# ScalarE writes x plus normed x, GpSimd adds the bias behind its gathers, and x2 is transposed at the end of the outer layer

## The chip, the cores and the metric

The kernel runs on one core of one Trainium2 chip. The metric is device time in microseconds (us); lower is better. The core's engines are TensorE (PE in the rows; PEld is its weight load), VectorE (DVE), ScalarE (ACT), GpSimd (POOL) and SyncE (SP), each with its own instruction stream, and they order themselves by semaphores. ACTq and SPq are the places where ScalarE and SyncE issue transfers.

## The reference

A graph layer and then a mixture-of-experts layer run over 6250 nodes of 256 features and 100000 edges of 96 features, all in float32:

```python
# graph layer, on xn = layernorm(x)
out1 = segment_sum(edge_attr, dst);  out2 = segment_max(edge_attr, dst) (0 where a node has no edge)
out3 = out1 / max(count, 1)
h = concat([xn, out1, out2, out3, u[0]])
x = x + (relu(h @ W1 + b1) @ W2 + b2) + xn
# expert layer, on x2 = layernorm(x): 16 experts, the best two by x2 @ gate_w + gate_b
x = x + layernorm(x2 + moe(x2)) * gamma + beta
```

The part that matters here is the sum behind the graph layer: for each node row it adds the product with W2, the bias b2, the row x and its normed row xn.

## The kernel before

Three stages follow each other. In the first, DVE scans the edges in ten chunks, each 96 + 96 scans, and SyncE stores the running sums and maxima of a chunk to DRAM. In the second, the outer layer, the 6250 nodes are taken in 25 macro steps of 250 nodes (two tiles of 125 rows), from the last node to the first. The third routes the nodes and runs 113 expert tiles. The first and second overlap: macro step i needs the chunks that hold the last edges of its nodes, and the semaphore chunk_done says how many are stored.

Each engine runs a macro step as a hand-written order of helper calls, and what it works on differs from engine to engine:

- PE, gnn_step(i): layer1(i) in two halves of four hidden blocks (lines 969, 971, 973), with router(i-2) between the halves (line 1002); turn(i+1), which transposes the inputs of the next step (lines 950, 953); layer2(i), 32 + 32 recorded matmul rows for its two tiles (line 983), with turn_x2(i-1), four transposes (line 995), between the tiles.
- ACT, gnn_step(i): store_x1(i-1), which waits for the finished rows; moments1(i+1), the mean and deviation of the next x (lines 734, 739); carry_in(i+1), the scaling and masks of what the gathers brought (lines 717 to 725); relu(i, 0) (line 769); take_logits(i-2) (line 810); moments2(i-1) (lines 778, 783); the issue of the load of x for step i+2 (line 743); mask_rows(i+1), which ends with the normed x in XN (lines 749 to 755); relu(i, 1); take_turned(i+1); write_x2(i-1) and its store (lines 791, 801); take_x2(i-1) (line 806); take_g(i), which copies layer2's result out of PSUM (line 817).
- POOL, rows_step(i): add_rows(i-1), GO = GO + RES (line 549); residual(i), which is RES = XN + x (line 566) and then RES = RES + b2 (line 568); cut(i+1) (line 527); norm1(i+1) (lines 540 to 544); join(i+1) (lines 531 to 535); norm2(i-1) (lines 554 to 559); gather(i+2), an index copy (line 512) and six indirect transfers (lines 520 to 522).

RES is one buffer. XN, XR (the raw x) and the gathered tiles have two buffers each. PE's wait that matters most below is in the second half of layer1(i), which takes over the PSUM banks that relu(i, 0) has read:

```python
if q:
    pe.wait_ge(h_ready, (i + 1) * HC + n + 1)
```

Of the kernel before, what the change touches and what calls it, by code (L numbers as in the profile page):

```python
# [21 lines left out]
ALU = mybir.AluOpType  # L22
ACT = mybir.ActivationFunctionType
# [59 lines left out]
def after(i, g, b, n=1):  # L83

    return i + n, g + (b + n) // 2, (b + n) % 2


def gnn_moe_kernel(nc, x, dst, edge_attr, u, gW1, gb1, gW2, gb2, gate_w, gate_b,
# [5 lines left out]
    NX, _, FF = ew1.shape  # L94
    NT = 125
    TILES = N // NT
    MACROS = TILES // 2
# [58 lines left out]
    with ExitStack() as ctx:  # L156
        def sem(name):
            return ctx.enter_context(nc.semaphore(name))
# [7 lines left out]
        k = Area(mem, 0, KEPT)  # L166
# [22 lines left out]
        wsel = k.take(2, TILES, parts=NT)  # L189
        IX = k.take(TILES, 2, parts=NT, dt=U32)  # L190
        rowU = k.take(TILES, parts=NT, dt=U32)
        mean1, dev_1, rstd_1, nmr_1 = (k.take(2, parts=NT) for _ in range(4))
        Lo = k.take(TILES, NX, parts=NT)
        gatef = k.take(MACROS, parts=1)
        gatei = k.take(MACROS, parts=1, dt=I32)
# [128 lines left out]
        pick_step = sem("pick_step")  # L324
        ix_copied, carried, joined, node_rows = sem("ix_copied"), sem("carried"), sem("joined"), sem("node_rows")
        xr_got = [sem(f"xr_got{i}") for i in range(2)]
        residual_ready, x1_ready = sem("residual_ready"), sem("x1_ready")
        moments2_step, norm2_step, rstd2_ready = sem("moments2_step"), sem("norm2_step"), sem("norm2_rstd_ready")
        turned, turned_out = sem("turned"), sem("turned_out")
        h_psum, h_ready, g_psum, g_out = sem("h_psum"), sem("h_ready"), sem("g_psum"), sem("g_out")  # L330
# [138 lines left out]
        def _(pool):  # L469
# [39 lines left out]
            def gather(i, g, b):  # L509
                level = pool.value_load(gatei[0:1, bass.ds(MACROS - 1 - i, 1)], min_val=1, max_val=LEVELS)  # L510
                hold(pool, turned, i + 1)
                pool.tensor_copy(IXn[b], IX[:, bass.ds(2 * (MACROS - 1 - i), 2), :]).then_inc(ix_copied, 1)
                pool.wait_ge(ix_copied, i + 1)
                hold(pool, chunk_done, level * LEVEL)
                for lv in range(1, LEVELS + 1):
                    edges, pieces = lv * LEVEL * P * T, lv * LEVEL * P
                    with pool.If(level == lv):
                        for a in range(2):
                            last, before = (bass.IndirectOffsetOnAxis(IXn[b][:, a, n:n + 1], 0) for n in range(2))
                            pool.indirect_dma_start(out=GM[b][:, a, :], out_offset=None, in_=s_max[0:edges], in_offset=last).then_inc(gathered[b], 16)  # L520
                            pool.indirect_dma_start(out=GS[b][:, a, :], out_offset=None, in_=s_sum[0:edges], in_offset=last).then_inc(gathered[b], 16)
                            pool.indirect_dma_start(out=GC[b][:, a, :], out_offset=None, in_=carry[0:pieces], in_offset=before).then_inc(gathered[b], 16)
# [11 lines left out]
                pool.wait_ge(picked, i + 1)  # L534
                pool.tensor_tensor(RAW[b][:, :, 1, :], take_c, take_p, ALU.add).then_inc(joined, 1)

            def norm1(i):
                s2 = Steps(pool, norm1_step, i * 2)
                hold(pool, moments1_step, i * 4 + 4)
                s2.mark(pool.tensor_scalar(dev_1, dev_1, 1.0 / D, EPS, ALU.mult, ALU.add))  # L540
                s2.wait()
                s2.mark(pool.tensor_tensor(rstd_1, dev_1, rpow, ALU.pow))
                s2.wait()
                pool.tensor_tensor(nmr_1, mean1, rstd_1, ALU.mult).then_inc(rstd1_ready, 1)

            def add_rows(i):
                pool.wait_ge(g_out, i + 2)
                pool.wait_ge(residual_ready, 2 * i + 2)
                pool.tensor_tensor(GO, GO, RES, ALU.add).then_inc(x1_ready, 1)

            def norm2(i):
# [6 lines left out]
                hold(pool, norm2_step, i * 2 + 2)  # L558
                pool.tensor_tensor(nmr_2[:, at], mean2, rstd_2[:, at], ALU.mult).then_inc(rstd2_ready, 1)

            def residual(i, g, b):
                if not isinstance(i, int) or i:
                    pool.wait_ge(x1_ready, i)
                pool.wait_ge(xr_got[b], (g + 1) * 16)
                pool.wait_ge(node_rows, i + 1)
                pool.tensor_tensor(RES, XN[b], XR[b][0:NT], ALU.add).then_inc(residual_ready, 1)
                pool.wait_ge(residual_ready, 2 * i + 1)
                pool.tensor_tensor(RES, RES, b2bc, ALU.add).then_inc(residual_ready, 1)

            def rows_step(i, g, b):  # L570
                more = not isinstance(i, int) or i + 1 < MACROS
                norm = not isinstance(i, int) or i >= 1
                if norm:
                    add_rows(i - 1)
                residual(i, g, b)
                if more:
                    cut(*after(i, g, b))
                    norm1(i + 1)
                    join(*after(i, g, b))
                if norm:  # L580
                    norm2(i - 1)
                if not isinstance(i, int) or i + 2 < MACROS:
                    gather(*after(i, g, b, 2))
            pool.sem_inc(joined, 1)
            gather(0, 0, 0)
            norm1(0)
            cut(0, 0, 0)
            join(0, 0, 0)
            gather(1, 0, 1)
# [62 lines left out]
        def _(act):  # L652
# [89 lines left out]
            def load_x(i, b):  # L742
                act.dma_start(XR[b], node_rows_of(MACROS - 1 - i)).then_inc(xr_got[b], 16)

            def mask_rows(i, g, b):
                act.wait_ge(joined, i + 2)
                for a in range(2):
                    j = bass.ds(2 * (MACROS - 1 - i) + a, 1)
                    act.activation(NB[b][:, a, 0:2 * EF], RAW[b][:, a, :, :].rearrange("p s f -> p (s f)"), ACT.Identity, scale=has[:, j])
                    act.activation(NB[b][:, a, 2 * EF:2 * P], RAW[b][:, a, 0, 0:EF - REST], ACT.Identity, scale=rch[:, j])  # L750
                    act.activation(NB[b][:, a, 2 * P:3 * P].rearrange("p (n r) -> p n r", n=QUAD), spread(RAW[b][:, a, 0, EF - REST:EF], 1, QUAD),
                                   ACT.Identity, scale=rch[:, j])
                act.wait_ge(rstd1_ready, i + 1)
                for a in range(2):
                    ins = act.activation(XN[b][:, a, :], XR[b][0:NT, a, :], ACT.Identity, bias=nmr_1[:, a:a + 1], scale=rstd_1[:, a:a + 1])  # L755
                ins.then_inc(node_rows, 1)

            def take_turned(i, g, b):
                act.wait_ge(turned, i + 3)
# [39 lines left out]
            def store_x2(i):  # L799
                act.wait_ge(x2_rows, i + 1)  # L800
                act.dma_start(by_pair(x2_d)[bass.ds(MACROS - 1 - i, 1)], X2p).then_inc(x2_st, 16)
# [18 lines left out]
            def gnn_step(i, g, b):  # L820
                more = not isinstance(i, int) or i + 1 < MACROS
                norm = not isinstance(i, int) or i >= 1
                logit = not isinstance(i, int) or i >= 2
                if norm:
                    store_x1(i - 1)
                if more:
                    moments1(*after(i, g, b), 0)
                    moments1(*after(i, g, b), 1)
                    carry_in(*after(i, g, b))
                relu(i, 0)  # L830
                if logit:
                    take_logits(i - 2)
                if norm:
                    moments2(i - 1, 0)
                    moments2(i - 1, 1)
                if not isinstance(i, int) or i + 2 < MACROS:
                    act.wait_ge(residual_ready, 2 * i + 2)
                    load_x(i + 2, b)
                if more:
                    mask_rows(*after(i, g, b))  # L840
                relu(i, 1)
                if more:
                    take_turned(*after(i, g, b))
                if norm:
                    write_x2(i - 1)
                    store_x2(i - 1)
                    take_x2(i - 1)
                take_g(i, g, b)
            moments1(0, 0, 0, 0)
            moments1(0, 0, 0, 1)  # L850
            act.wait_ge(index_ready, 1)
# [66 lines left out]
        def _(pe):  # L918
# [56 lines left out]
                    if between and q == 0:  # L975
                        between()

            def layer2(i, g, b, between=None):
                for a in range(2):
                    for hc in range(HC):  # L980
                        if a == 0 and (hc == 0 or hc > QUAD):
                            pe.wait_ge(h_ready, (i + 1) * HC + max(hc, QUAD) + 1)
                        ins = pe.matmul(bank(5, a * D, (a + 1) * D, NT), H[:, hc, a * NT:(a + 1) * NT], W2[:, hc, :], start=(hc == 0), stop=(hc == HC - 1))  # L983
                    if between and a == 0:
                        between()
                ins.then_inc(g_psum, 1)

            def turn_x2(r):
# [17 lines left out]
            def gnn_step(i, g, b):  # L1006
                layer1(i, g, b, (lambda: router(i - 2)) if not isinstance(i, int) or i >= 2 else None)
                if not isinstance(i, int) or i + 1 < MACROS:
                    turn(*after(i, g, b))
                layer2(i, g, b, (lambda: turn_x2(i - 1)) if not isinstance(i, int) or i >= 1 else None)  # L1010
            turn(0, 0, 0)
            gnn_step(0, 0, 0)
            gnn_step(1, 0, 1)
# [398 lines left out]
```

## Time and profile before

| | us |
|---|---|
| median of three runs | 1420.55 |
| lowest and highest of them | 1414.31, 1423.67 |
| the profiled execution | 1423.21 |
| its span, first to last instruction | 1421.5 |
| PE, DVE, ACT, POOL busy | 1201.3, 848.0, 645.1, 795.2 |
| outer layer, first PE transpose to last router | 121.82 to about 789 |

The first row is the time that a change is held against; the profiled execution is one run, 2.7 us above it, and 1.7 us of it lie outside its span. The busy sums run over stages with different limits, so they don't say what a macro step waits for. This is read from the order of the rows within a step.

### The profile page before, as it was taken

To read this page: it belongs to the slowest core of one execution; us is meant where nothing else is said; L and a number is where in the kernel's file an instruction comes from. 1 tells how busy PE (TensorE), PEld (TensorE's weight loads), DVE (VectorE), ACT (ScalarE), POOL (GpSimd) and SP (SyncE) were. 2 spreads that over 40 slices of the span, in tenths; PEclk is the share of its full clock that TensorE was granted. 3 is DMA by queue.
4 is the path that set the end of the run, shared out by engine and by line. 5 is a ranking of instruction groups with operands and counts; after the bars stand their busy time and mean duration, and the time that the engine had idled before them with its cause. 6 is when DMAs were issued, how large, how long until landed. Compare 5 with 4: busy or idle time off the path is not lost.

```text
span 1421.5 us, 28692 instructions
## 1 busy us (share of the span) xinstructions
PE 1201.3 (85%) x6677; PEld 1015.0 (71%) x6678; DVE 848.0 (60%) x3007; ACT 645.1 (45%) x1969; POOL 795.2 (56%) x1060
## 2 busy tenths in 40 slices
PE   2004998998998999999998254999999999999798
PEld 1003887887887788788887144999999999998343
DVE  5999999999999899000000695344444344443796
ACT  5853555656656556566563000332323232323453
POOL 4874565665665566666751001676766777765122
PEclk7556999999999999999999577999999999999555
DMA  9976677676676656611110823122221222222883
GB/s 314 300 227 246 232 268 268 265 276 262 258 281 260 230 186 236 196 45 42 58 34 30 278 85 133 62 69 74 69 71 63 75 69 71 69 72 58 297 284 102
DMA packets 87468, 231.48 MB, mean 163 GB/s; under 512 B 22145, under 2 KB 34819, under 8 KB 87285
## 3 DMA queue, kind: packets, MB, share of 16 engines
q1 hardware_dynamic: 50401, 167.53, 32.5%
q0 software_dynamic: 26048, 43.47, 10.5%
q10 hardware_dynamic: 10964, 19.96, 4.0%
q14 instruction: 47, 0.39, 0.1%
q8 instruction: 8, 0.13, 0.0%
HBM read 116.42 MB, written 114.25 MB: 162 GB/s over the span
## 4 chain that ended last, share of the span: by engine, by line
PE 54%; DVE 33%; DMA 4%; issue 4%; POOL 2%; ACT 1%; DVEq 1%; SPq 0%; POOLq 0%; ACTq 0%
PE ps L1061 14%; PE ps L1069 14%; DVE mem L1142 12%; DVE mem L1146 12%; PE ps L983 5%; PE ps L969 5%; PE ps L971 5%; PE ps L1089 3%; PE ps L1091 3%; PE ps L1048 2%; DVE mem L1162 2%; DVE mem L1283 1%; DMA mem<-piece_carry,mem 1%; DMA mem<-in_edge_attr_dram 1%; DVE mem L1167 1%
## 5 line engine op out<-in xcount | busy, mean ns | idle before, releaser
L879 ACT ACTIVATE mem<-ps,mem 128x128 f32<-128x128 f32 x452 | 128.8, 368 | 374.8 <-PE ps L1061 374.8
L969 PE MATMUL ps<-mem 128*128 128x250 f32 x800 | 214.1, 391 | 27.2 <-ACT mem L769 25.7
L1061 PEld LDWEIGHTS ps<-mem 128*128 128x128 f32 x1808 | 221.8, 194 | 5.7
L1061 PE MATMUL ps<-mem 128*128 128x128 f32 x1808 | 222.2, 277 | 0.0
L1069 PE MATMUL ps<-mem 128*128 x904 | 213.8, 379 | 0.4 <-issue 0.4
L1142 DVE TENSOR_TENSOR_SCAN mem<-ps,mem 128x80 f32<-128x80 f32 x960 | 207.9, 303 | 0.3
L971 PE MATMUL ps<-mem 128*128 128x250 f32 x800 | 208.1, 383 | 0.0
L1146 DVE TENSOR_TENSOR_SCAN mem<-ps,mem 128x80 f32<-128x80 f32 x960 | 207.8, 308 | 0.0
L621 POOL DMA_INDIRECT expert_rows<-mem x113 | 138.2, 1223 | 113.3 <-DVE mem L1317 66.0
L969 PEld LDWEIGHTS ps<-mem 128*128 128x128 f32 x800 | 156.2, 198 | 47.5 <-ACT mem L769 27.4
L983 PE MATMUL ps<-mem 128*125 128x256 f32 x800 | 180.9, 379 | 0.7 <-ACT mem L769 0.7
L1069 PEld LDWEIGHTS ps<-mem 128*128 128x128 f32 x904 | 163.0, 190 | 18.3 <-issue 0.7
L971 PEld LDWEIGHTS ps<-mem 128*128 128x128 f32 x800 | 156.8, 196 | 19.8
L983 PEld LDWEIGHTS ps<-mem 128*125 128x125 f32 x800 | 146.2, 188 | 21.0 <-ACT mem L769 1.1
L1317 DVE TENSOR_TENSOR mem<-ps,mem 128x256 f32<-128x256 f32 x113 | 47.9, 424 | 170.0 <-PE ps L1069 166.9
L1310 DVE COPY mem<-mem 128x1024 f32 x113 | 78.4, 694 | 85.0 <-issue 81.8
L1232 DVE TENSOR_TENSOR mem<-mem 125x800 f32<-125x800 f32 x1 | 1.0, 994 | 214.0 <-ACT mem L810 214.0
L615 POOL DMA_INDIRECT mem<-x_normed,mem x113 | 113.4, 1004 | 24.1 <-issue 16.9
L950 PE MATMUL ps<-mem 125*128 125x125 f32 x100 | 20.7, 289 | 94.4 <-ACT mem L755 94.4
L769 ACT ACTIVATE mem<-ps,mem 128x250 f32<-128x250 f32 x200 | 77.0, 467 | 49.9 <-PE ps L973 49.8
L520 POOL DMA_INDIRECT mem<-run_max,mem x50 | 63.3, 1265 | 47.3 <-issue 43.6
L950 PEld LDWEIGHTS ps<-mem 125*128 125x128 f32 x100 | 11.5, 144 | 102.2 <-issue 102.2
(206 smaller groups left out, 1785.6 us busy)
## 6 DMA issues: line engine op xcount, KB each, us to landing
run_sum<-mem SPq DMA_DIRECT2D x40, 960.0 KB
run_max<-mem SPq DMA_DIRECT2D x40, 960.0 KB, 7.6
mem<-in_edge_attr_dram SPq DMA_DIRECT2D x36, 960.0 KB, 10.3
mem<-in_L_ffn_w_dram SPq DMA_DIRECT2D x32, 512.0 KB, 9.7
mem<-expert_rows SPq DMA_DIRECT2D x22, 512.0 KB, 6.0
x_rows<-mem ACTq DMA_DIRECT2D x25, 256.0 KB, 2.0
x_normed<-mem ACTq DMA_DIRECT2D x25, 256.0 KB, 2.8
mem<-in_x_dram ACTq DMA_DIRECT2D x24, 256.0 KB, 7.8
```

Source lines behind the costliest of these rows:

```text
L615: pool.indirect_dma_start(out=XG[b], out_offset=None, in_=x2_d, in_offset=bass.IndirectOffsetOnAxis(slot_now[b], 0)).then_inc(xg_got[b], 16)
L621: pool.indirect_dma_start(out=ya_d, out_offset=bass.IndirectOffsetOnAxis(into_now[b], 0), in_=YO[b], in_offset=None).then_inc(yo_stored[b] ...
L769: act.activation(H[:, hc, :], bank(H_BANKS[q][hc - q * QUAD], 0, M), ACT.Relu, bias=cbias[:, hc:hc + 1]).then_inc(h_ready, 1)
L879: ins = act.activation(hT[b][:, c, :], bank(2 + b, c * P, (c + 1) * P), ACT.Relu, bias=eb1c[:, bass.ds(e, 1), c])
L969: pe.matmul(h, W1x[:, c, hc * P:(hc + 1) * P], XT[b][:, c, :], start=(c == 0), stop=False)
L971: pe.matmul(h, W1a[:, s, hc * P:(hc + 1) * P], AT[b][:, s, :], start=False, stop=False)
L983: ins = pe.matmul(bank(5, a * D, (a + 1) * D, NT), H[:, hc, a * NT:(a + 1) * NT], W2[:, hc, :], start=(hc == 0), stop=(hc == HC - 1))
L1061: ins = pe.matmul(bank(2 + b, f * P, (f + 1) * P), w1now[b][:, c, f * P:(f + 1) * P], XgT[b][:, c, :], start=(c == 0), stop=(c == DC - 1))
L1069: ins = pe.matmul(bank(6 + b, 0, D), hT[b][:, c, :], w(c * D, D), start=(c == 0), stop=(c == FC - 1))
L1142: ins = dve.tensor_tensor_scan(out=Sb[:, ::-1, f], data0=keep[b][:, ::-1], data1=Eb[b][:, ::-1, f], initial=0.0, op0=ALU.mult, op1=ALU.add)
L1146: ins = dve.tensor_tensor_scan(out=Eb[b][:, ::-1, f], data0=bound[b][:, ::-1], data1=Eb[b][:, ::-1, f], initial=-FMAX, op0=ALU.min, op1=AL ...
L1310: dve.tensor_copy(w1now[b].rearrange("p c f -> p (c f)"), wexp[:, bass.ds(e, 1), 0:DC * FF].rearrange("p o w -> p (o w)")).then_inc(w1_sta ...
```

## The change

Three edits act together. ScalarE gets a new helper, twice(i), which writes RES = x * (1 + rstd) + shift in one pass for each tile, that is x plus normed x; GpSimd's norm1 supplies 1 + rstd with one more small instruction, and its factors are kept in two buffers. GpSimd's residual(i) shrinks to the bias add, and it moves from ahead of cut(i+1) to the end of rows_step(i), behind gather(i+2). PE's turn_x2(i-1) moves from between the two tiles of layer2(i) to behind it, and ScalarE takes layer2's result before x2's. ScalarE's issue of the load of x moves from ahead of mask_rows(i+1) to behind relu(i, 1).

```diff
-                pool.tensor_tensor(nmr_1, mean1, rstd_1, ALU.mult).then_inc(rstd1_ready, 1)
+                pool.tensor_tensor(shift_1[:, b], mean1, rstd_1[:, b], ALU.mult)
+                pool.tensor_scalar(twice_1[:, b], rstd_1[:, b], 1.0, None, ALU.add).then_inc(rstd1_ready, 1)
...
             def add_rows(i):
                 pool.wait_ge(g_out, i + 2)
-                pool.wait_ge(residual_ready, 2 * i + 2)
+                pool.wait_ge(residual_ready, i + 1)
                 pool.tensor_tensor(GO, GO, RES, ALU.add).then_inc(x1_ready, 1)
...
-            def residual(i, g, b):
-                if not isinstance(i, int) or i:
-                    pool.wait_ge(x1_ready, i)
-                pool.wait_ge(xr_got[b], (g + 1) * 16)
-                pool.wait_ge(node_rows, i + 1)
-                pool.tensor_tensor(RES, XN[b], XR[b][0:NT], ALU.add).then_inc(residual_ready, 1)
-                pool.wait_ge(residual_ready, 2 * i + 1)
+            def residual(i):
+                pool.wait_ge(twice_rows, i + 1)
                 pool.tensor_tensor(RES, RES, b2bc, ALU.add).then_inc(residual_ready, 1)
...
                     add_rows(i - 1)
-                residual(i, g, b)
                 if more:
                     cut(*after(i, g, b))
-                    norm1(i + 1)
+                    norm1(i + 1, 1 - b)
                     join(*after(i, g, b))
                 if norm:
                     norm2(i - 1)
                 if not isinstance(i, int) or i + 2 < MACROS:
                     gather(*after(i, g, b, 2))
+                residual(i)
...
+            def twice(i, b):
+                if not isinstance(i, int) or i:
+                    act.wait_ge(x1_ready, i)
+                for a in range(2):
+                    ins = act.activation(RES[:, a, :], XR[b][0:NT, a, :], ACT.Identity, bias=shift_1[:, b, a:a + 1], scale=twice_1[:, b, a:a + 1])
+                ins.then_inc(twice_rows, 1)
...
-                if not isinstance(i, int) or i + 2 < MACROS:
-                    act.wait_ge(residual_ready, 2 * i + 2)
-                    load_x(i + 2, b)
+                twice(i, b)
                 if more:
                     mask_rows(*after(i, g, b))
                 relu(i, 1)
+                if not isinstance(i, int) or i + 2 < MACROS:
+                    act.wait_ge(twice_rows, i + 1)
+                    load_x(i + 2, b)
                 if more:
                     take_turned(*after(i, g, b))
                 if norm:
                     write_x2(i - 1)
                     store_x2(i - 1)
+                take_g(i, g, b)
+                if norm:
                     take_x2(i - 1)
-                take_g(i, g, b)
...
-                layer2(i, g, b, (lambda: turn_x2(i - 1)) if not isinstance(i, int) or i >= 1 else None)
+                layer2(i, g, b)
+                if not isinstance(i, int) or i >= 1:
+                    turn_x2(i - 1)
```

## Rows read from the trace of the kernel before

**Rows 1.** Windows: busy us and instructions of PE, PEld, DVE, ACT, POOL; PEclk; DMA; GB/s.

```profile
660.00:770.00 110.00, 109.27 (x604) 92.92 (x603) 0.00 (x0) 66.11 (x200) 58.89 (x81) 1.00 0.12 37
```

**Rows 2.** Timeline, one macro step: start us, us, engine, line, [idle before].

```profile
651.90 3.62 PE L983 MATMUL ps<-mem 128*125 128x256 f32 x16
...
663.77 1.11 PE L969 MATMUL ps<-mem 128*128 128x250 f32 x4
...
671.36 0.43 PE L950 MATMUL ps<-mem 125*128 125x125 f32 x2
...
675.94 0.59 PE L995 MATMUL ps<-mem 125*128 125x125 f32 x4
...
676.37 3.62 PE L983 MATMUL ps<-mem 128*125 128x256 f32 x16
```

**Rows 3.** Timeline, the same step on POOL and ACT.

```profile
656.55 1.28 POOL L549 TENSOR_TENSOR mem<-mem 125x512 f32<-125x512 f32 x1
...
658.69 0.42 ACT L734 ACTIVATE mem<-mem 125x256 f32<-125x256 f32 x1 [2.37 <-POOL mem L549]
...
662.91 0.46 ACT L725 ACTIVATE mem<-mem 125x192 f32<-125x192 f32 x1
...
663.27 1.52 ACT L769 ACTIVATE mem<-ps,mem 128x250 f32<-128x250 f32 x4
...
666.90 0.19 ACT L783 ACTIVATION_READ_ACCUMULATOR mem<-mem 125x1 f32 x1
...
667.28 0.19 POOL L554 TENSOR_SCALAR mem<-mem 125x2 f32<-125x2 f32 x1 [1.49 <-ACT mem L783]
...
668.02 0.45 ACT L749 ACTIVATE mem<-mem 125x192 f32<-125x192 f32 x1 [0.93 <-ACT mem L783]
...
669.78 1.08 ACT L755 ACTIVATE mem<-mem 125x256 f32<-125x256 f32 x2
...
672.15 1.33 POOL L520 DMA_INDIRECT mem<-run_max,mem  x1 [2.07 <-issue]
...
679.84 1.21 POOL L522 DMA_INDIRECT mem<-piece_carry,mem  x1 [0.30 <-issue]
...
680.13 0.66 ACT L817 ACTIVATE mem<-ps 125x256 f32<-125x256 f32 x2 [2.97 <-PE ps L983]
...
681.06 1.28 POOL L549 TENSOR_TENSOR mem<-mem 125x512 f32<-125x512 f32 x1
```

**Rows 4.** Groups by line, 125 to 820 us: busy us, mean ns, idle before.

```profile
L566 POOL TENSOR_TENSOR mem<-mem 125x512 f32<-125x512 f32 x25 | 32.1, 1284 | 3.5 <-POOL mem L549 2.4
...
L568 POOL TENSOR_TENSOR mem<-mem 125x512 f32<-125x512 f32 x25 | 27.3, 1091 | 2.0
```

**Rows 5.** Timeline of POOL and ACT, other macro steps.

```profile
504.91 1.28 POOL L549 TENSOR_TENSOR mem<-mem 125x512 f32<-125x512 f32 x1 [2.09 <-ACT mem L817]
...
579.85 1.29 POOL L549 TENSOR_TENSOR mem<-mem 125x512 f32<-125x512 f32 x1
...
586.16 0.59 POOL L527 TENSOR_TENSOR mem<-mem 125x192 f32<-125x192 f32 x1 [2.51 <-DMA mem<-piece_carry,mem]
...
606.84 0.66 ACT L817 ACTIVATE mem<-ps 125x256 f32<-125x256 f32 x2 [2.97 <-PE ps L983]
...
607.68 1.27 POOL L549 TENSOR_TENSOR mem<-mem 125x512 f32<-125x512 f32 x1 [1.67 <-ACT mem L817]
...
729.77 1.28 POOL L549 TENSOR_TENSOR mem<-mem 125x512 f32<-125x512 f32 x1
```

**Rows 6.** Timeline of PE, steps that begin with a wait.

```profile
376.43 1.11 PE L969 MATMUL ps<-mem 128*128 128x250 f32 x4 [0.79 <-ACT mem L769]
...
485.32 2.03 PE L969 MATMUL ps<-mem 128*128 128x250 f32 x4 [3.42 <-ACT mem L769]
...
588.80 1.69 PE L969 MATMUL ps<-mem 128*128 128x250 f32 x4 [1.95 <-ACT mem L769]
```

**Rows 7.** Line 743, the loads of x: issue to landing.

```profile
DMA to landing us min/median/max: 2.5/7.8/8.4
```

More of the change, by code:

```diff
@@ L191, in gnn_moe_kernel @@
         rowU = k.take(TILES, parts=NT, dt=U32)
-        mean1, dev_1, rstd_1, nmr_1 = (k.take(2, parts=NT) for _ in range(4))
+        mean1, dev_1 = (k.take(2, parts=NT) for _ in range(2))
+        rstd_1, twice_1, shift_1 = (k.take(2, 2, parts=NT) for _ in range(3))
         Lo = k.take(TILES, NX, parts=NT)
@@ L326, in gnn_moe_kernel @@
         xr_got = [sem(f"xr_got{i}") for i in range(2)]
-        residual_ready, x1_ready = sem("residual_ready"), sem("x1_ready")
+        twice_rows, residual_ready, x1_ready = sem("x_and_normed_x"), sem("residual_ready"), sem("x1_ready")
         moments2_step, norm2_step, rstd2_ready = sem("moments2_step"), sem("norm2_step"), sem("norm2_rstd_ready")
@@ L535, in join, with norm1 @@
                 pool.tensor_tensor(RAW[b][:, :, 1, :], take_c, take_p, ALU.add).then_inc(joined, 1)
-            def norm1(i):
+            def norm1(i, b):
                 s2 = Steps(pool, norm1_step, i * 2)
@@ L541, in norm1 @@
                 s2.wait()
-                s2.mark(pool.tensor_tensor(rstd_1, dev_1, rpow, ALU.pow))
+                s2.mark(pool.tensor_tensor(rstd_1[:, b], dev_1, rpow, ALU.pow))
                 s2.wait()
-                pool.tensor_tensor(nmr_1, mean1, rstd_1, ALU.mult).then_inc(rstd1_ready, 1)
+                pool.tensor_tensor(shift_1[:, b], mean1, rstd_1[:, b], ALU.mult)
+                pool.tensor_scalar(twice_1[:, b], rstd_1[:, b], 1.0, None, ALU.add).then_inc(rstd1_ready, 1)
             def add_rows(i):
                 pool.wait_ge(g_out, i + 2)
-                pool.wait_ge(residual_ready, 2 * i + 2)
+                pool.wait_ge(residual_ready, i + 1)
                 pool.tensor_tensor(GO, GO, RES, ALU.add).then_inc(x1_ready, 1)
@@ L583, in rows_step @@
                     gather(*after(i, g, b, 2))
+                residual(i)
             pool.sem_inc(joined, 1)
             gather(0, 0, 0)
-            norm1(0)
+            norm1(0, 0)
             cut(0, 0, 0)
@@ L754, in mask_rows @@
                 for a in range(2):
-                    ins = act.activation(XN[b][:, a, :], XR[b][0:NT, a, :], ACT.Identity, bias=nmr_1[:, a:a + 1], scale=rstd_1[:, a:a + 1])
+                    ins = act.activation(XN[b][:, a, :], XR[b][0:NT, a, :], ACT.Identity, bias=shift_1[:, b, a:a + 1], scale=rstd_1[:, b, a:a + 1])
                 ins.then_inc(node_rows, 1)
+            def twice(i, b):
[4 more added lines that the diff above has]
+                ins.then_inc(twice_rows, 1)
             def take_turned(i, g, b):
@@ L976, in layer1, with layer2 @@
                         between()
-            def layer2(i, g, b, between=None):
+            def layer2(i, g, b):
                 for a in range(2):
@@ L983, in layer2 @@
                         ins = pe.matmul(bank(5, a * D, (a + 1) * D, NT), H[:, hc, a * NT:(a + 1) * NT], W2[:, hc, :], start=(hc == 0), stop=(hc == HC - 1))
-                    if between and a == 0:
-                        between()
                 ins.then_inc(g_psum, 1)
```

## The prediction

> **What bounds the kernel now.** I read the chain of waits and the windows first, then the groups by line, then the timeline of single macro steps, because the change touches only the outer layer. In its quiet part PE is busy for 109.27 of 110 us at the full clock [rows 1], and the same matmul comes again after 24.47 us (676.37 - 651.90) [rows 2]. So the layer looks bound by PE, at some 24.4 us for a macro step.
>
> The timeline shows a second loop of the same length, and it is the one to look at. It runs through POOL and ACT [rows 3]: add_rows starts at 656.55; ACT waits for it and starts moments1 at 658.69; from there ACT has no wait through carry_in (its last row at 662.91), relu(i, 0) at 663.27, and moments2, which ends at 667.09; POOL waits for exactly that and starts norm2 at 667.28; the gather follows, its six transfers from 672.15 to 681.05; and add_rows starts again at 681.06. That makes 24.51 us, and the last link is the queue of POOL itself: line 549 starts 0.01 us after line 522 ends. take_g, the other thing that it waits for, ended at 680.79; where add_rows does wait for it, it starts 0.18 us after its end (607.68 - 606.84 - 0.66) [rows 5], which would have been 680.97. So the two loops are tied within 0.1 us here, and the one through POOL is the later by a hair. That it binds at times is seen in PE's short waits for relu(i, 0), such as 0.79 us [rows 6]. The old residual, lines 566 and 568, lies in that loop's shadow: POOL does it while ACT does moments1 and carry_in, and POOL then still waits for ACT, 1.49 us before line 554 [rows 3].
>
> Until about 590 us a third thing counts: in seven macro steps the gathered rows land late, while the chunks are stored and loaded, and POOL and ACT wait for the transfer, 2.51 us at 586.16 among them [rows 5]. PE then waits too, 1.95 us in that step and 3.42 us in another [rows 6].
>
> **The change, part by part.**
>
> 1. Removed: line 566, 25 of them at 1.28 us [rows 4]. All of it lies beside ACT's part of the loop. Gain on the loop: 0. Cut(i+1) starts 2.4 us sooner, but what it feeds, ACT's masks, comes behind moments1 anyway, and there the row shows no wait for it.
>
> 2. Moved: the bias add, 1.09 us [rows 4], from that shadow to the place between the end of the gather and the next add_rows, where POOL has no idle time at all [rows 3]. With the drained wait that add_rows(i) now has on it (0.08 us lies between lines 566 and 568, 0.24 between 549 and 566), that is 1.09 + 0.1 = 1.19 us on the loop, 1.4 at most. Queued behind it: add_rows(i), and through x1_ready ACT's store_x1, moments1, carry_in and relu(i+1, 0), for which PE waits in the second half of layer1. Its own wait, on twice(i), is over 12 us old by then and costs nothing. At least it costs 0, if the transfers' spans on POOL end in time that another instruction could use.
>
> What the rows show here is that POOL starts line 549 only when line 522 is through. The Trainium skill has the rule for it, on the page "TensorE: Matmul & The Clock Gate", section "Architectural detail: the array is 16× 32×32, not 1× 128×128": GpSimd takes its queue strictly in order, so nothing behind a slow instruction overtakes it. The trace agrees (0.01 us between lines 522 and 549). By that rule the add costs its full 1.19 us in each turn; were the transfers issued aside, it would cost 0.
>
> 3. Added on ACT: twice(i), two passes of the shape of line 755, 1.08 us [rows 3]. They stand behind moments2, so outside the loop. They take the place of the gap of 0.93 us in which ACT issued the load of x. Mask_rows starts some 0.2 to 0.3 us later; XN is ready at 670.86 and PE transposes it from 671.36 [rows 2, 3], so 0.5 us of cover less about 0.1 for the semaphore hides it. Without that cover it would cost 0.3 us of PE, which in the lengthened loop has over 1 us to spare. The small add in norm1, about 0.2 us like line 554, is again in POOL's shadow: 0.
>
> 4. The load of x: issued after relu(i, 1), some 6 us later, at about 673.5. It lands 7.8 us later in the median, 8.4 at most [rows 7], by 681.9; the moments that need it started at 683.1 and will start later. Cost 0 in quiet steps. Its issue (0.4 to 0.6 us) now delays take_turned, which PE needs only behind layer2, 7 us on: 0.
>
> 5. turn_x2 behind layer2: PE's work is the same. Layer2 ends 0.43 us sooner (676.37 - 675.94), take_g with it, and add_rows where that was what it waited for. Worth 0.43 us once, since POOL is then the late one, and nothing in each step.
>
> **The sum.** The loop goes from 24.5 to 25.7 us, and PE gets about 1.2 us of idle time in a step. In the stretch behind the edge chunks five turns with a gather lie between 607.68 and 729.77 [rows 5] (the mean is 24.42): 5 x 1.19 = +5.95. Before 590 us, the loop waits for transfers whose time the chunks set. Such a step restarts both loops: after it add_rows waits for take_g, as by 1.67 and 2.09 us [rows 5], and the added 1.19 fits there. Three turns from 504.91 to 579.85 add 3 x 1.19 - 0.43 = 3.1; the turn from 579.85 to 607.68 took 27.83 and without a late transfer it needs 24.5 + 1.19 = 25.7, so the lag behind it is 3.1 + 25.7 - 27.83 = 1.0. I take 1.0 + 5.95 less 0.43 for the last layer2 = +6.5 us. The last three steps have no gather and run by PE. The routing and expert stages are untouched: 0. On the profiled execution that is 1423.2 + 6.5 = 1429.7; against the median, 1420.55 + 6.5 = 1427.
>
> Bounds: if the late transfers move along with the gathers instead of standing fixed in time, each restart takes up only its slack, and the same ledger with 1.19 gives +9, with 1.4 it gives +12. With 0 on the loop it gives -0.5 to -2.
>
> **The rivals.**
>
> A. The loop doesn't lengthen (the spans of indirect transfers hide time, or the tie at 680.97 against 681.05 means that POOL has slack that I don't see). Then nothing changes but the 0.43 us: 1419 to 1421. Against it speaks the turn from 504.91 to 579.85, three of 24.98 us on average [rows 5], over PE's own 24.47, with no late transfer in them: the loop through POOL was the longer one.
>
> B. Slower: PE's new idle time costs its clock. After 0.79 us of waiting the matmuls ran at 1.11 us for four; after 1.95 us at 1.69, and after 3.42 us at 2.03 [rows 6], the level of 1.2 instead of 2.4 GHz. The new wait of 1.2 us lies between. If in every turn it costs as after the 3.42 us, where add_rows came 19.6 us after the matmul of 485.32 [rows 5, 6] instead of 17.3 [rows 2, 3], a step takes 7.2 (663.77 - 656.55) + 19.6 - 0.4 = 26.4 instead of 25.7: +0.7 in each of some 20 turns, 14 us more, +20 in all: 1441. It decides once the loss is over the 1.2 to 1.6 us that PE has to spare. The Trainium skill, same page, section "What's actually happening", says that the clock gate follows how busy PE has recently been; it leaves this case open, and the rows of 0.79 and 1.95 us are the nearest.
>
> C. Faster: the late transfers depend on the meeting of a gather and a chunk's traffic, every 52 to 55 us. Two turns now take 51.4 us instead of 49, so the meetings shift. If none of them met, the ledger ends at -7: 1413. A gain of over 14 us would need the waits gone and no longer loop as well.
>
> D. The same meeting in the other direction: two more late steps of 4 to 6 us each: +16: 1437.
>
> **How the numbers follow.** Forecast (+2 to +12) 0.60; A 0.15; C 0.10; B 0.07; D 0.08. The likeliest is 1427. The range of 8 in 10 takes the forecast with its bounds, A and half of C, and adds the 3 us by which a median of few runs moves: 1415 to 1438. Faster or slower by over 1% (14.2 us, about what a measurement here can tell from no change) are part of C and the noise, 0.05, and B with part of D and of the upper bound, 0.13; within 1%: 0.82.
>
> **What would show it.** In the changed profile: a bias add of 1.09 us on POOL right behind the last line of the gather and, within 0.1 us, add_rows; starts of add_rows 25.6 to 25.7 us apart behind 607 us (step 2); PE waiting about 1.2 us for relu(i, 0) in those steps, with a busy share near 95%; no wait of moments1 for x (step 4); none of the transposes for XN over 0.3 us (step 3); and the granted clock at 1.0 there (against B). I am wrong if the starts stay 24.4 us apart (A), if the waits for gathered rows change by more than 5 us in sum (C, D), or if ACT's added pass turns up between add_rows and relu(i, 0).

## The result, and the profile after

The changed kernel takes 1426.35 us in the median of 20 runs (1411.67 to 1429.59) against 1421.53 us of the kernel before in 20 runs beside it: a ratio of 1.0032, 95% interval 1.0017 to 1.0048, or 2.4 to 6.8 us. The forecast was 1427, 6.5 us over the median of that time.

The page of the changed kernel, its span and the busy time of each engine:

```profile
span 1424.0 us, 28727 instructions
...
PE 1205.9 (85%) x6677; PEld 1017.9 (71%) x6678; DVE 844.0 (59%) x3007; ACT 668.4 (47%) x2019; POOL 768.2 (54%) x1060
```

POOL has 27 us less to do than before, and ACT 23 us more: from the one 25 adds of 1.28 us are gone and a small instruction for each step has come, and the other has 50 more passes. The kernel is slower all the same. POOL's share shows work, not what others wait for, and that is in the timeline. POOL in the changed kernel, behind the edge chunks (start, duration, line; line 523 is the last transfer of a gather, 565 the bias add, 551 add_rows, 528 cut, 541 norm1, 556 norm2):

```profile
654.81 1.10 POOL L565 TENSOR_TENSOR mem<-mem 125x512 f32<-125x512 f32 x1
...
656.06 1.27 POOL L551 TENSOR_TENSOR mem<-mem 125x512 f32<-125x512 f32 x1
...
657.44 0.59 POOL L528 TENSOR_TENSOR mem<-mem 125x192 f32<-125x192 f32 x1
...
660.69 0.19 POOL L541 TENSOR_SCALAR mem<-mem 125x2 f32<-125x2 f32 x1 [2.66 <-ACT mem L736]
...
666.78 0.19 POOL L556 TENSOR_SCALAR mem<-mem 125x2 f32<-125x2 f32 x1 [1.48 <-ACT mem L787]
...
679.33 1.21 POOL L523 DMA_INDIRECT mem<-piece_carry,mem  x1 [0.30 <-issue]
...
680.57 1.10 POOL L565 TENSOR_TENSOR mem<-mem 125x512 f32<-125x512 f32 x1
...
681.82 1.27 POOL L551 TENSOR_TENSOR mem<-mem 125x512 f32<-125x512 f32 x1 [0.15 <-POOL mem L565]
```

This answers to [rows 3]. Read it from the end of the gather at 680.54: the add stands at 680.57 and add_rows at 681.82, so 1.28 us lie where 0.01 lay. The turn from 656.06 is 25.76 us long instead of 24.51. The time that the removed add has freed shows as a wait of 2.66 us for ACT ahead of line 541; the wait ahead of norm2 is what it was, 1.48 us. ACT shows what it waits for in each turn (line 821 is take_g, 731 moments1, 752 the end of mask_rows):

```profile
658.18 0.42 ACT L731 ACTIVATE mem<-mem 125x256 f32<-125x256 f32 x1 [3.58 <-POOL mem L551]
...
669.36 1.08 ACT L752 ACTIVATE mem<-mem 125x256 f32<-125x256 f32 x2
...
679.19 0.66 ACT L821 ACTIVATE mem<-ps 125x256 f32<-125x256 f32 x2 [4.37 <-PE ps L989]
```

take_g is done at 679.85, 1.97 us ahead of the add_rows that needs it; before, it was done 0.27 us ahead [rows 3]. And PE, which had no idle time in this part [rows 1], now waits for the relu of the first half (start, duration of four matmuls, the wait ahead):

```profile
611.45 1.99 PE L975 MATMUL ps<-mem 128*128 128x250 f32 x4 [0.98 <-ACT mem L773]
663.26 1.11 PE L975 MATMUL ps<-mem 128*128 128x250 f32 x4 [1.13 <-ACT mem L773]
688.87 1.11 PE L975 MATMUL ps<-mem 128*128 128x250 f32 x4 [1.02 <-ACT mem L773]
```

These are three of the five turns in this stretch. In the other two PE is the later one, and ACT's relu waits for it (start, duration, the wait ahead; line 979 ends the first half of layer1):

```profile
636.89 1.55 ACT L773 ACTIVATE mem<-ps,mem 128x250 f32<-128x250 f32 x4 [0.37 <-PE ps L979]
714.31 1.55 ACT L773 ACTIVATE mem<-ps,mem 128x250 f32<-128x250 f32 x4 [0.48 <-PE ps L979]
```

The last section comes back to these two.

The stretch of five turns in the windows view (us of the stretch, then busy us of PE, PEld, DVE, ACT, POOL, the granted clock, DMA, GB/s):

```profile
604.25:733.44 129.19, 126.06 (x672) 107.10 (x671) 0.00 (x0) 82.91 (x245) 76.02 (x106) 0.97 0.16 46
```

129.19 us for what took 729.77 - 607.68 = 122.09 before [rows 5]: 7.1 us more. The last two turns give 1.15 of it back (733.44 to 780.69 is 47.25, and 729.77 to 778.17 was 48.40), since no gather stands in them and add_rows can use the earlier result of layer2.

### The profile page after: what moved, and what is told of

The parts are those of the page before. It is cut to its first block, busy times and chain, and to the rows that moved or that the text cites. A ratio compares the mean times of both kernels' runs of the same rounds, so it can differ in the third digit from the quotient of the medians.

```text
span 1424.0 us, 28727 instructions
## 1 busy us (share of the span) xinstructions
PE 1205.9 (85%) x6677; PEld 1017.9 (71%) x6678; DVE 844.0 (59%) x3007; ACT 668.4 (47%) x2019; POOL 768.2 (54%) x1060
## 4 chain that ended last, share of the span: by engine, by line
PE 47%; DVE 33%; issue 7%; POOL 5%; DMA 4%; ACT 3%; DVEq 1%; POOLq 1%; ACTq 0%; SPq 0%
PE ps L1067 14%; PE ps L1075 14%; DVE mem L1148 12%; DVE mem L1152 12%; PE ps L1095 3%; PE ps L1097 3%; PE ps L975 3%; PE ps L989 3%; PE ps L977 3%; PE ps L1054 2%; DVE mem L1168 1%; DVE mem L1289 1%; POOL mem L521 1%; POOL mem L522 1%; DVE mem L1163 1%
## 5 line engine op out<-in xcount | busy, mean ns | idle before, releaser
L975 PE MATMUL ps<-mem 128*128 128x250 f32 x800 | 216.5, 395 | 29.7 <-ACT mem L773 28.3
L977 PE MATMUL ps<-mem 128*128 128x250 f32 x800 | 210.7, 387 | 0.0
L989 PE MATMUL ps<-mem 128*125 128x256 f32 x800 | 176.9, 379 | 0.7 <-ACT mem L773 0.7
```

The costliest lines, as they stand in the source:

```text
L975: pe.matmul(h, W1x[:, c, hc * P:(hc + 1) * P], XT[b][:, c, :], start=(c == 0), stop=False)
L977: pe.matmul(h, W1a[:, s, hc * P:(hc + 1) * P], AT[b][:, s, :], start=False, stop=False)
```

## The experiments

Each kernel is compared with the kernel before on the same chip: e1, e2, e4 and e5 on one (8 to 12 runs each, against 31), e3, e6, e7 and e8 on another (4 runs of e3, 11 of the others, against 27). So kernels of different chips are held against each other by their ratios. In the table, "turn 17" is the start of the eighteenth add_rows, the first in the quiet stretch, and "five turns" the time from it to the twenty-third, both from one profiled execution of each kernel.

| kernel | median us | ratio to before, 95% | turn 17 | five turns |
|---|---|---|---|---|
| before | 1421.53 | 1 | 607.68 | 122.09 |
| changed | 1426.35 | 1.0032 (1.0017 to 1.0048) | 604.25 | 129.19 |
| e1, add in the shadow | 1419.59 | 0.9984 (0.9974 to 0.9994) | 603.74 | 122.76 |
| e2, no add | 1420.28 | 0.9982 (0.9970 to 0.9993) | 604.19 | 122.69 |
| e3, add made twice | 1437.25 | 1.0124 (1.0089 to 1.0160) | 616.57 | 133.71 |
| e4, order of x2 alone | 1421.0 | 0.9987 (0.9972 to 1.0001) | 605.77 | 122.11 |
| e5, add moved alone | 1427.65 | 1.0040 (1.0024 to 1.0057) | 607.19 | 127.75 |
| e6, behind gathers to step 15 | 1420.64 | 1.0002 (0.9986 to 1.0019) | 607.15 | 122.78 |
| e7, behind gathers from step 16 | 1424.1 | 1.0034 (1.0017 to 1.0050) | 604.95 | 128.63 |
| e8, ScalarE's pass on the loop | 1426.98 | 1.0044 (1.0026 to 1.0061) | 607.85 | 128.13 |

**e1: the same work, in the shadow.**

```diff
-        RES = a.take(2, D, parts=NT)
+        RES = [a.take(2, D, parts=NT) for _ in range(2)]
...
                 if norm:
-                    add_rows(i - 1)
+                    add_rows(i - 1, 1 - b)
+                residual(i, b)
                 if more:
                     cut(*after(i, g, b))
...
                     gather(*after(i, g, b, 2))
-                residual(i)
...
-                twice(i, b)
                 if more:
+                    twice(i + 1, 1 - b)
                     mask_rows(*after(i, g, b))
...
                     act.wait_ge(twice_rows, i + 1)
+                    act.wait_ge(node_rows, i + 1)
                     load_x(i + 2, b)
```

> The changed kernel with two buffers for x plus normed x: ScalarE's pass for step i+1 is made in step i, and GpSimd's bias add stands right behind add_rows, in the time in which it waits for ScalarE. All else as changed. If the loop through GpSimd's queue is the cause (theory 1), the five turns of add_rows behind the last late transfer fall from 129.2 us back to 122.1 to 122.7, PE's waits of 1 us there go, and the time is 1419 to 1422, about 5 to 7 us under the changed kernel. If ScalarE's added pass or its new order is the cause (theory 2), the pass is still there and the turns stay near 129 us, the time near 1426. If late transfers made the difference (theory 3), the five turns and the time part ways: turns at 122 and a time anywhere from 1413 to 1430.

The timeline of POOL in e1:

```profile
676.54 1.21 POOL L523 DMA_INDIRECT mem<-piece_carry,mem  x1 [0.30 <-issue]
677.78 1.28 POOL L551 TENSOR_TENSOR mem<-mem 125x512 f32<-125x512 f32 x1
679.01 1.09 POOL L565 TENSOR_TENSOR mem<-mem 125x512 f32<-125x512 f32 x1
...
682.35 0.19 POOL L541 TENSOR_SCALAR mem<-mem 125x2 f32<-125x2 f32 x1 [1.54 <-ACT mem L736]
```

The add takes the same 1.09 us, now behind add_rows, and ends in POOL's wait for ACT, which is still 1.54 us long. The turns are back to 24.55 us on average, and five of them take 122.76 us, just over the stated 122.7. ScalarE makes the same passes as in the changed kernel, so they aren't the cause. The time lies 0.48% (6.8 us) under the changed kernel's by the two ratios, and under the kernel before too. One thing is new: at 474.70 moments1 waits 2.16 us for the load of x, which the changed kernel never does. e6, e7 and e8, which have the two buffers as well, wait there too, 2.6 to 3.0 us.

**e2: no add.**

```diff
                 pool.wait_ge(twice_rows, i + 1)
-                pool.tensor_tensor(RES, RES, b2bc, ALU.add).then_inc(residual_ready, 1)
+                pool.sem_inc(residual_ready, 1)
```

> The changed kernel with the bias add left out (the output lacks b2; its waits and its count stay, and the place is the same). Theory 1: 1.2 us less in each turn, five turns in 122.1 to 123.3 us, time 1419 to 1422, as with the add in the shadow. Theory 2: five turns at about 129, time near 1426.

To leave the add out is worth no more than to put it into the shadow: 122.69 against 122.76 us for five turns, ratios of 0.9982 and 0.9984. So in e1 the add costs nothing that can be measured, and in the changed kernel it costs at least all that the change loses, since without it the kernel is faster than the one before.

**e5: only the add moved.**

```diff
                 pool.tensor_tensor(RES, XN[b], XR[b][0:NT], ALU.add).then_inc(residual_ready, 1)
+
+            def bias(i):
                 pool.wait_ge(residual_ready, 2 * i + 1)
                 pool.tensor_tensor(RES, RES, b2bc, ALU.add).then_inc(residual_ready, 1)
...
                     gather(*after(i, g, b, 2))
+                bias(i)
...
-                    act.wait_ge(residual_ready, 2 * i + 2)
+                    act.wait_ge(residual_ready, 2 * i + 1)
                     load_x(i + 2, b)
```

> The kernel before with one thing changed: the bias add, and it alone, stands behind the gathers; x plus normed x is still added by GpSimd in the old place, ScalarE makes no added pass, PE's order is the old one. Theory 1: the five turns need 128 to 129.5 us and the time is 4 to 7 us over the kernel before, as the whole change. Theory 2: no change against the kernel before, within 1 us, and turns of 24.4 us.

POOL in e5 (line 570 is the moved add, 566 the old one of x and normed x):

```profile
681.59 1.21 POOL L522 DMA_INDIRECT mem<-piece_carry,mem  x1 [0.31 <-issue]
682.83 1.10 POOL L570 TENSOR_TENSOR mem<-mem 125x512 f32<-125x512 f32 x1
684.01 1.26 POOL L549 TENSOR_TENSOR mem<-mem 125x512 f32<-125x512 f32 x1
685.35 1.27 POOL L566 TENSOR_TENSOR mem<-mem 125x512 f32<-125x512 f32 x1
```

This one edit reproduces the loss: 1.0040 against 1.0032, within each other's interval. A turn is 25.55 us, 1.13 over that of before, and the five take 127.75 us, a little under the stated 128. PE waits 0.76 to 1.18 us in each of the five turns.

**e4: only the order of x2.**

```diff
-                layer2(i, g, b, (lambda: turn_x2(i - 1)) if not isinstance(i, int) or i >= 1 else None)
+                layer2(i, g, b)
+                if not isinstance(i, int) or i >= 1:
+                    turn_x2(i - 1)
...
                     store_x2(i - 1)
+                take_g(i, g, b)
+                if norm:
                     take_x2(i - 1)
-                take_g(i, g, b)
```

> The kernel before with the order of PE and of ScalarE's take_x2 alone changed: x2 is transposed behind layer2, and layer2's result is taken first. Theory 1: the result comes 0.4 us sooner, which the loop through GpSimd can use only where it waits for it: between 0 and -2 us against the kernel before, turns of 24.4 us. If that order cost something by itself (x2 taken later, the router late), it would be over +2 us here.

1.8 us less (interval 4 less to 0.1 more), with turns as before. The sign is that of the 0.43 us that each restart can use, but the interval ends at 1.0001, so this part is not shown to help, only not to cost.

**e6 and e7: where in the layer the loss arises.** Both are e1 with the add behind the gathers in one part of the macro steps:

```diff
+                if not behind:
+                    residual(i, b)
...
                     gather(*after(i, g, b, 2))
+                if behind:
+                    residual(i, b)
...
-            in_pairs(pool, MACROS, rows_step, ahead=3, first=2)
+            in_pairs(pool, 16, lambda i, g, b: rows_step(i, g, b, EARLY), first=2)
+            in_pairs(pool, MACROS, lambda i, g, b: rows_step(i, g, b, LATE), ahead=3, first=16)
```

(EARLY and LATE are True and False in e6, False and True in e7; steps 0 and 1 go with EARLY.)

> The kernel with the two buffers (e1), but in the macro steps 0 to 15 the bias add stands behind the gathers, as in the changed kernel, and from step 16 on in the shadow. If late transfers at fixed times set the pace of the early steps (theory 1), the 1.2 us in each of 16 turns is taken up there: add_rows of turn 17 starts where it does in e1, within 1.5 us, and the time is that of e1, 1419 to 1422. If the delay adds up (rival), 16 x 1.2 us less the slack of the restarts is 8 to 15 us more: 1428 to 1435.

> The mirror of e6: in the shadow up to step 15, behind the gathers from step 16 on. Theory 1: nearly all of the change's loss is here: five turns in 127.5 to 129.5 us, time 5 to 8 us over e1, 1425 to 1428. Rival: 7 of 23 turns carry about a third of the loss, 2 to 3 us over e1.

e7 is 5.0 in 1000 (7.1 us) over e1 by the ratios, e6 1.8 in 1000 (2.6 us), and each ratio is known to about 2 us. The median of e7, 1424.1, is 4.5 us over e1's on another chip and just under the stated range; its five turns are inside theirs. So the steps from 16 on carry most of the loss and the sixteen before them little.

e6 missed its stated 1.5 us: turn 17 starts 3.4 us later than in e1. The rows tell where this arises. Turn 13 still starts at 501.54, against 501.32 in e1. Up to there the late rows follow the chunks: cut starts behind them at 318.4, 372.3, 426.7 and 480.3 in e1 and at 318.3, 370.8, 424.6 and 479.5 in e6, where the last load of edges was issued 1 us sooner (461.42 for 462.37). That is the absorption which the ledger assumed. It ends with the last late transfer. POOL in e1, then in e6, with the end of that gather and the wait for its rows in brackets:

```profile
575.23 1.21 POOL L523 DMA_INDIRECT mem<-piece_carry,mem  x1 [0.30 <-issue]
...
582.75 0.59 POOL L528 TENSOR_TENSOR mem<-mem 125x192 f32<-125x192 f32 x1 [3.96 <-DMA mem<-piece_carry,mem]
```

```profile
577.36 1.21 POOL L523 DMA_INDIRECT mem<-piece_carry,mem  x1 [0.30 <-issue]
...
584.95 0.59 POOL L528 TENSOR_TENSOR mem<-mem 125x192 f32<-125x192 f32 x1 [4.04 <-DMA mem<-piece_carry,mem]
```

Cut starts 6.31 us behind the end of the gather in e1 and 6.38 in e6. In every kernel but e3 this time is 5.9 to 6.5 us, though the gather ends anywhere from 576.4 to 580.2. Nothing that SyncE issues there shifts the same way: in e6 the last chunk's last store is issued 1.3 us sooner than in e1 (564.13 for 565.44), and the last of the early loads of expert weights 2.2 us sooner (573.15 for 575.39). So this transfer moves with its gather and carries on the lag of 2.1 us that has built up since turn 13. What makes it late is not shown. The other 1.2 us lie between it and turn 17, where PE had a granted clock of 0.85 in e6 and of 0.92 in e1, and add_rows waits for layer2's result.

**e3: the point where it ends.**

```diff
                 pool.tensor_tensor(RES, RES, b2bc, ALU.add).then_inc(residual_ready, 1)
+                pool.wait_ge(residual_ready, 2 * i + 1)
+                pool.tensor_tensor(RES, RES, b2bc, ALU.add).then_inc(residual_ready, 1)
```

> The changed kernel with the bias added twice behind the gathers (the output has 2 b2). Theory 1: one more 1.2 us in each turn, five turns in 134.5 to 136 us. Two turns now need about 54 us, as long as a chunk, so the early part has little left that takes it up, and the total is 6 us more from the tail and 0 to 6 from the early part: 1432 to 1439. If GpSimd had room behind the gathers after all, the time stays at 1426.

POOL in e3:

```profile
694.62 1.10 POOL L565 TENSOR_TENSOR mem<-mem 125x512 f32<-125x512 f32 x1
695.80 1.09 POOL L567 TENSOR_TENSOR mem<-mem 125x512 f32<-125x512 f32 x1
696.97 1.27 POOL L551 TENSOR_TENSOR mem<-mem 125x512 f32<-125x512 f32 x1
```

The gather ended at 694.59, so 2.38 us now lie between it and add_rows. A turn takes 26.74 us, and the five 133.71, under the stated 134.5 to 136. By the ratios the second add costs almost three times what the whole change did: 9.2 in 1000 on top of 3.2. Turn 17 starts at 616.57, nine to thirteen us later than in all other kernels. In its early part every turn is 26 to 28 us long, and behind 200 us POOL waits over 1 us for three gathers only, where e6 has six such waits. Two turns are now as long as the 54 us between chunks, so the waits for the chunks no longer hide the loop.

**e8: not GpSimd's queue alone, but the loop.**

```diff
                     take_logits(i - 2)
+                if more:
+                    twice(i + 1, 1 - b)
                 if norm:
                     moments2(i - 1, 0)
...
                 if more:
-                    twice(i + 1, 1 - b)
                     mask_rows(*after(i, g, b))
```

> The kernel with the two buffers (e1), with ScalarE's pass for x plus normed x moved by one place, from behind moments2 to ahead of it; GpSimd's add stays in its shadow. Theory 1 says that the loop runs through ScalarE from moments1 to moments2, so the 1.1 us of the pass now lie on it: five turns in 127 to 129 us, time 4 to 7 us over e1, though no engine has more work. If only GpSimd's queue is the limit and ScalarE has room, the time is that of e1.

ACT in e8 (774 is the relu, 815 take_logits, 760 the pass, 783 the first of moments2):

```profile
665.84 1.53 ACT L774 ACTIVATE mem<-ps,mem 128x250 f32<-128x250 f32 x4
667.25 0.21 ACT L815 ACTIVATE mem<-ps 125x32 f32 x1
667.32 1.11 ACT L760 ACTIVATE mem<-mem 125x256 f32<-125x256 f32 x2
668.31 0.43 ACT L783 ACTIVATE mem<-mem 125x256 f32<-125x256 f32 x1
```

The pass moved by one place, from behind moments2 to ahead of it, costs 6.0 in 1000 against e1, 8.5 us, known to some 3, where 4 to 7 were expected. Five turns take 128.13 us, 1.07 more each, which is the pass itself. ACT is 47% busy in the changed kernel, and there is no room for one microsecond between moments1 and moments2.

## Why the prediction was right

**The bound.** Two loops of one length, tied, with the one through POOL's queue the later: right. e2 and e5 each changed one thing, e1 and e8 differ only in the place of ScalarE's pass, and all four answered as this says.

**Step 1, the removed add, worth 0:** right for the loop. POOL waits for ACT in its place (2.66 us ahead of line 541). Beside the loop it may be worth something (the chunks, below).

**Step 2, the moved add, 1.19 us a turn, 5.95 us for five:** the mechanism was right and the size a little low. From the end of the gather to add_rows it is 1.28 us. The five turns grew by 1.22, 1.72, 1.25, 1.24 and 1.67, in sum 7.1 us. Three of them show the add and its waits; the second and the fifth have some 0.45 more, which is PE's clock (last section). e5, with the add alone and a granted clock of 1.00, gives 1.13 each. The last two turns gave 1.15 back where the ledger had 0.43, so the sum behind turn 17 is 5.95 against 5.52 expected.

**The early steps, +1.0:** the ledger's own terms came out, but not the point from which it counted. From turn 13 to turn 16 the three turns took 78.03 us instead of 74.94, so +3.09 for the 3.1 expected. The next took 25.89 instead of 27.83, so -1.94 for -2.1. But turn 13 itself started at 500.33 instead of 504.91, 4.58 us sooner, since the chunks came sooner: the last load of edges was issued at 460.40 instead of 465.00. The ledger had no such term. So turn 17 starts at 604.25, 3.43 us sooner than before, and not 1.0 later.

**The number.** In the two profiled executions the terms are -4.58 + 3.09 - 1.94 + 7.10 - 1.15 = +2.5 us, which is the difference of their spans, 1424.0 and 1421.5. The medians differ by 4.8 us, and the forecast was +6.5. That it came so close is in part luck: the turns grew by more than forecast, and the earlier chunks made up for it.

**Step 3, ScalarE's pass, 0:** right. XN is ready at 670.44 (669.36 + 1.08) and PE transposes it from 670.86 without a wait. e1 makes the same pass one step ahead and is faster than the kernel before.

**Step 4, the later load of x, 0:** right. moments1 waited for POOL's line 551 and never for x: 62.9 of its 63.7 us of idle time, and no transfer is named for the rest. With two buffers it is not quite 0: the one wait of 2.16 us in e1.

**Step 5, x2 behind layer2:** unclear, 0 to 4 us of gain by e4; it didn't cost.

**The rivals.** A fell: the starts are 25.8 us apart. B fell as to its price of 0.7 us in every turn, but its mechanism is there: the granted clock over the five turns was 0.97 and not 1.0, and it cost some 0.9 us in sum (last section). PE was busy for 97.6% of them, more than the 95% expected, because of its slower matmuls. The sign for C and D came: behind 200 us POOL's waits for gathered rows grew from 23.9 to 36.4 us and ACT's fell from 21.0 to 15.2, +6.7 in sum, with a seventh late step at 262.25. It carries little weight, since POOL now reaches cut 2.4 us sooner in each of these steps and waits that much longer for the same rows. PE's waits for relu(i, 0) up to 600 us went from 20.4 to 22.4 us only. Turn 17 came within 4.2 us of the same place in all kernels but e3.

**The version to take** is e1: 1419.59 us, 0.16% under the kernel before (0.06 to 0.26%) and 0.48% under the changed one. It keeps the whole of the change but for where the add stands, at the price of one more buffer.

## What to carry to other kernels

Move work by where it lies on the loop, not by which engine is less busy: an engine at 54% had no 1.2 us to give behind its gathers, and had over 2 us behind add_rows. To find the loop, follow one buffer around once and note where each wait is zero; where two loops are within 0.1 us of each other, as here, nothing hides an addition to the later one: 1.20 us more in POOL's queue made each turn of e5 1.13 us longer. Where an outside clock, such as chunks that arrive at fixed times, stretches some turns, an addition is nearly free there, as up to turn 13 in e6, until the turns fill the time between arrivals, and then it costs in every turn, as in e3. A wait for a transfer is no such clock by itself: the last late one here moved with its gather.

## What the runs showed that was not expected

**PE's clock can fall after a wait of one microsecond.** In the changed kernel the wait of 0.98 us at 611.45 was followed by four matmuls in 1.99 us, and the longer one of 1.13 us at 663.26 by four in 1.11. After the wait of 1.02 us at 688.87 the first four took 1.11 us and the next ones longer:

```profile
689.82 1.65 PE L977 MATMUL ps<-mem 128*128 128x250 f32 x4
691.27 1.87 PE L975 MATMUL ps<-mem 128*128 128x250 f32 x4
```

The windows around the first two places, then those of the five turns, with the granted clock in the third column from the right:

```profile
611.00:618.00 7.00, 6.55 (x23) 5.60 (x24) 0.00 (x0) 6.87 (x23) 3.56 (x8) 0.76 0.00 0
663.00:670.00 7.00, 6.74 (x32) 5.98 (x32) 0.00 (x0) 6.87 (x23) 3.50 (x8) 1.00 0.00 0
```

```profile
604.25:629.88 25.63, 24.65 (x128) 20.67 (x127) 0.00 (x0) 16.22 (x49) 15.21 (x21) 0.93 0.14 46
629.88:656.06 26.18, 26.18 (x144) 22.49 (x143) 0.00 (x0) 16.96 (x50) 15.22 (x22) 1.00 0.16 46
656.06:681.82 25.76, 24.63 (x136) 20.99 (x135) 0.00 (x0) 16.54 (x49) 15.19 (x21) 1.00 0.16 45
681.82:707.66 25.84, 24.82 (x128) 20.85 (x128) 0.00 (x0) 16.53 (x49) 15.20 (x21) 0.93 0.16 46
707.66:733.44 25.78, 25.78 (x142) 22.10 (x141) 0.00 (x0) 16.64 (x49) 15.21 (x22) 1.00 0.16 46
```

0.76 is a mean of stretches at 2.4 and at 1.2 GHz. The turns with the slower clock, the first and the fourth, are not longer for it. The loss comes one turn later: PE is behind, has no idle time left, and relu(i, 0) waits for it, 0.37 us at 636.89 and 0.48 us at 714.31. These are the two turns that grew by 1.7 us where the others grew by 1.24, so the clock cost some 0.9 us in five turns. PE's new idle time didn't hide it.

**The chunks came sooner.** SyncE's last store of sums, before and in the changed kernel:

```profile
539.53 3.09 SPq L394 DMA_DIRECT2D run_sum<-mem  x4
```

```profile
534.48 3.08 SPq L395 DMA_DIRECT2D run_sum<-mem  x4
```

In e4 and e5, which like the kernel before add x and normed x on GpSimd, it stands at 538.84 and 538.80. In the other six it stands at 535.52 to 537.59. One group of DVE's scans, before and in the changed kernel up to 600 us, took 4.1 us less:

```profile
L1162 DVE TENSOR_TENSOR_SCAN mem<-mem 32x128 f32<-32x128 f32 x60 | 32.6, 591 | 1.8 <-DVE mem L1157 1.4
```

```profile
L1168 DVE TENSOR_TENSOR_SCAN mem<-mem 32x128 f32<-32x128 f32 x60 | 28.5, 523 | 1.8 <-DVE mem L1163 1.4
```

So the add that was worth nothing on the loop may have held up the chunks. This rests on one trace of each kernel, and no experiment aimed at it: the cause is open, and that group alone doesn't explain it (35.3 us in e4, 30.6 in e5, 26.5 to 30.5 in the other six). It may also be part of why e1 is faster than the kernel before.
